# Rotary embedding in a local-attention layer: the two products added by paired transposes into PSUM, and the copy of the last 32 key columns made by ScalarE

## The reference, cut to what matters

```
q, k, v = split(shift(x) @ Wqkv)                  # 16 heads of 64
q = l2norm(q) * q_scale;  k = l2norm(k) * k_scale
q = q * cos * scale + rotate_half(q) * sin * scale
k = k * cos / scale + rotate_half(k) * sin / scale
# windows of 32 tokens; each sees its own keys and those of the window before
sim  = (q @ [k_before, k]^T) * 8, masked;  attn = softmax(sim)
out  = attn @ [v_before, v];  x = out @ Wo + x
```

## Time and profile before

| | |
|---|---|
| median of 3 runs | 5173.48 us (5169.82 to 5185.4) |
| the profiled execution, its own time | 5172.85 us |
| its span, first to last instruction | 5170.8 us |
| PE busy | 3934.8 us (76%) |
| DVE busy | 4374.4 us (85%) |
| ACT busy | 3040.4 us (59%) |
| POOL busy | 2537.9 us (49%) |
| mean granted TensorE clock | 0.913 |

### The profile page before, as it was taken

The page is one execution under the profiler, slowest core; times in us unless marked ns, Lnnn a source line. Parts: engine busy times, 40 slices in busy tenths (PEclk is TensorE's granted clock), DMA queues, the critical chain, the costliest instruction groups (busy, mean ns, idle before and its releaser), DMA issues. The chain is left out here.

```text
span 5170.8 us, 110439 instructions
## 1 busy us (share of the span) xinstructions
PE 3934.8 (76%) x39280; PEld 2903.7 (56%) x39280; DVE 4374.4 (85%) x7725; ACT 3040.4 (59%) x4888; POOL 2537.9 (49%) x1612
## 2 busy tenths in 40 slices
PE   5777777777777777767858678777787787777787
PEld 4655655656656646625535466466465565565565
DVE  8988989979979979954335399799799899898897
ACT  4765756746747747722413477477476476575575
POOL 5645646636636636611010266366366365464562
PEclk8988999989989989986978899899899998899899
DMA  1000000000000000021030000000000000000000
GB/s 47 8 23 11 7 22 12 8 27 6 7 27 7 8 25 8 8 62 26 2 74 1 33 7 7 26 8 21 13 8 20 14 8 19 15 7 22 12 7 12
DMA packets 30608, 88.57 MB, mean 17 GB/s; under 512 B 7505, under 2 KB 13649, under 8 KB 28369
## 3 DMA queue, kind: packets, MB, share of 16 engines
q1 hardware_dynamic: 29104, 80.95, 5.9%
q10 hardware_dynamic: 1152, 3.15, 0.2%
HBM read 38.72 MB, written 1.05 MB: 8 GB/s over the span
## 5 line engine op out<-in xcount | busy, mean ns | idle before, releaser
L771 POOL TENSOR_TENSOR pool<-pool 128x512 f32<-128x512 f32 x768 | 1069.1, 1413 | 968.3 <-DVE pool L869 968.3
L776 POOL TENSOR_TENSOR pool<-pool 128x1024 f32<-128x1024 f32 x384 | 1072.8, 2794 | 168.0 <-DVE pool L880 147.2
L443 PE MATMUL psum<-squares,pool 128*128 128x128 f32 x3072 | 475.4, 304 | 420.8 <-POOL pool L776 259.9
L443 PEld LDWEIGHTS psum<-squares,pool 128*128 128x128 f32 x3072 | 368.9, 153 | 587.2 <-issue 338.1
L880 DVE TENSOR_TENSOR pool<-pool 128x1024 f32<-128x1024 f32 x384 | 678.6, 1806 | 6.8
L483 PE MATMUL psum<-wqkv_hi,xs_lo 128*128 128x512 f32 x1152 | 522.2, 453 | 200.3 <-DVE pool L849 104.6
L646 ACT COPY pool<-psum 64x512 f32<-64x512 f32 x768 | 447.1, 582 | 367.1 <-PE psum L443 361.7
L474 PE MATMUL psum<-pool 128*64 128x128 f32 x6144 | 560.7, 296 | 116.7 <-ACT pool L661 116.5
L420 PE MATMUL psum<-pool 128*128 128x128 f32 x3072 | 455.4, 309 | 130.2 <-ACT pool L646 129.8
L859 DVE TENSOR_REDUCE pool<-pool 128x16 f32<-128x1024 f32 x384 | 449.9, 1210 | 88.1 <-ACT pool L685 88.0
L420 PEld LDWEIGHTS psum<-pool 128*128 128x128 f32 x3072 | 420.4, 219 | 179.4 <-ACT pool L646 167.8
(11 more groups left out here) (165 smaller groups left out, 8247.6 us busy)
## 6 DMA issues: line engine op xcount, KB each, us to landing
pool<-pool SPq DMA_DIRECT2D x192, 128.0 KB, 2.3
pool<-in_wqkv SPq DMA_DIRECT2D x12, 1536.0 KB, 6.0
k_st<-turn_st SPq DMA_DIRECT2D x8, 1536.0 KB, 21.3
pool<-in_wo SPq DMA_DIRECT2D x12, 512.0 KB, 3.6
pool<-in_w SPq DMA_DIRECT2D x12, 341.0 KB, 3.0
pool<-in_w SPq DMA_DIRECT2D x12, 192.0 KB, 2.9
rotary<-in_rotary SPq DMA_DIRECT2D x2, 1024.0 KB, 5.4
pool<-in_scale SPq DMA_DIRECT2D x12, 128.0 KB, 6.2
```

The costliest lines, as they stand in the source:

```text
L443: last = pe.transpose(bank(7 - p % 2)[:, P * j:P * j + P], rot[:, p // 2, 2 * c:2 * c + 2, :], ident)
L771: last = g.tensor_tensor(rot[:, q, :, hd * r:hd * r + hd], qn[:, q, :, hd * (1 - r):hd * (2 - r)], tab, ALU.mult)
L776: g.tensor_tensor(rot[:, q], rot[:, q], by_cos[:, q], ALU.add).then_inc(rot_ready, 1)
```

## The change

The add L776 and the tile `rot` go. GpSimd writes its product to a tile `by_sin`, `by_cos` stays as it was, and TensorE transposes both, the first with `start=True, stop=False` and the second with `start=False, stop=True` on the same 128x128 square of PSUM, so that the square holds the sum. That is 32 transposes in a unit in place of 16. The waits move with it: the transposes wait for `sin_ready` and `cos_ready` in place of `rot_ready`, and VectorE's L880 waits for `t_ready` of the unit before (its transposes of the same half) in place of `rot_ready`. GpSimd's L753 becomes a copy on ScalarE, behind its wait for `t_ready` of `p` = 2 and ahead of the first L646, and GpSimd's `keep` goes, with its wait for `s_ready`.

```diff
                             U = V0 + k
-                            pe.wait_ge(rot_ready, done(U, 2, 0))
+                            pe.wait_ge(sin_ready, done(U, 2, 0))
+                            pe.wait_ge(cos_ready, done(U, 2, 0))
...
-                                    pe.wait_ge(rot_ready, done(U, 2, 1))
+                                    pe.wait_ge(sin_ready, done(U, 2, 1))
+                                    pe.wait_ge(cos_ready, done(U, 2, 1))
...
-                                    last = pe.transpose(bank(7 - p % 2)[:, P * j:P * j + P],
-                                                        rot[:, p // 2, 2 * c:2 * c + 2, :], ident)
+                                    o = bank(7 - p % 2)[:, P * j:P * j + P]
+                                    pe.matmul(o, by_cos[:, p // 2, 2 * c:2 * c + 2, :], ident,
+                                              start=True, stop=False, is_transpose=True)
+                                    last = pe.matmul(o, by_sin[:, p // 2, 2 * c:2 * c + 2, :], ident,
+                                                     start=False, stop=True, is_transpose=True)
...
                                 if p == 2:
+                                    b = kT[k % 2]
+                                    a.copy(b[:, :, :, 0:WIN], b[:, :, :, P:P + WIN]).then_inc(k_kept, 1)
                                     a.wait_ge(k_kept, done(U))
...
-                        def keep(U, k):
-
-                            g.wait_ge(s_ready, done(U - 2))
-                            b = kT[k % 2]
-                            plain(g)
-                            g.tensor_copy(b[:, :, :, 0:WIN], b[:, :, :, P:P + WIN]).then_inc(k_kept, 1)
-
...
-                            if has(1):
-                                keep(U - 1, k - 1)
...
-                                        last = g.tensor_tensor(rot[:, q, :, hd * r:hd * r + hd],
+                                        last = g.tensor_tensor(by_sin[:, q, :, hd * r:hd * r + hd],
                                                                qn[:, q, :, hd * (1 - r):hd * (2 - r)], tab, ALU.mult)
                                     last.then_inc(sin_ready, 1)
-                                    g.wait_ge(sin_ready, done(U, 2, q))
-                                    g.wait_ge(cos_ready, done(U, 2, q))
-                                    g.tensor_tensor(rot[:, q], rot[:, q], by_cos[:, q], ALU.add).then_inc(rot_ready, 1)
...
-                        keep(U0 + UNITS - 1, UNITS - 1)
...
-                                v.wait_ge(rot_ready, done(U - 1, 2, 1))
                                 for q in range(2):
+                                    v.wait_ge(t_ready, done(U - 1, 4, 2 * q + 1))
```

More of the change, by code:

```diff
@@ L61, in macaron_program @@
         sq_ready, qn_ready, cos_ready = sem("sq_ready"), sem("qn_ready"), sem("cos_ready")
-        sin_ready, rot_ready, turn_ready = sem("sin_ready"), sem("rot_ready"), sem("turn_ready")
+        sin_ready, turn_ready = sem("sin_ready"), sem("turn_ready")
         t_ready, t_out, v_out = sem("t_ready"), sem("t_out"), sem("v_out")
@@ L95, in macaron_program @@
                        rb_ready, w1_ready, w2_ready],
-            "scalar": [xs_ready, sq_ready, v_out, t_out, p_ready, pt_ready, o_out, fsq_ready, gel_ready],
+            "scalar": [xs_ready, sq_ready, v_out, t_out, p_ready, pt_ready, o_out, fsq_ready, gel_ready, k_kept],
             "vector": [qn_ready, cos_ready, s_taken, block_ready, y_ready, norm_step, soft_step,
                        xc_ready, diag_ready, xn_ready, hid_ready, x_ready, var_step, aff_step],
-            "gpsimd": [lo_ready, w_hi, w_split, sin_ready, rot_ready, turn_ready, k_kept],
+            "gpsimd": [lo_ready, w_hi, w_split, sin_ready, turn_ready],
         }
@@ L270, in window_half @@
             by_cos = cut(2, HEADS, DH)
-            rot = cut(2, HEADS, DH)
+            by_sin = cut(2, HEADS, DH)
             ss = cut(2 * HEADS)
```

## The result

| | before | after |
|---|---|---|
| median of 4 runs each | 5177.23 us | 4953.28 us (4937.71 to 4975.03) |
| ratio | 1 | 0.957, 95% interval 0.953 to 0.961 |
| span of the profiled execution | 5170.8 us | 4949.2 us |
| DVE, PE, ACT, POOL busy | 4374, 3935, 3040, 2538 us | 4143, 4058, 3174, 1663 us |
| mean granted clock | 0.913 | 0.951 |

Faster by 4.3%, where 2.7% (5033 us) was forecast; the median lies 17 us under the lower end of the range. The lines have other numbers in the kernel after: L869, L880, L771, L846, L849, L859, L896 of before are L863, L874, L769, L840, L843, L853, L890 after; L443 is L446 and L448; L639, L646, L666, L673, L685 are L644, L653, L673, L680, L692; the key copy is L649.

A forecast was written before the change was run, and what follows sets the result against it. VectorE's instruction sequence was taken to bound the kernel. Full steps -8.4, start -5.8 and end +2.5 gave -11.7 us a layer, x12 = -140: 5033 us (-2.7%), range 4970 to 5110.

The forecast's parts named there:

- L145's wait for L776: VectorE's L145, held until GpSimd's sum L776 ends, falls to 0.18 us: -1.6 us a full step.
- the turns: GpSimd's L771 and VectorE's L880 alternate, so L880's pair takes 4.5 us instead of 3.43: +1.1 a full step.
- the start: A layer's first units, without L776's waits: unit 2's L869 comes 5.8 us earlier a layer.
- the slow pace: Transposes at 8 in 1.97 us, as in the layer's second step; unit 0's 32 were priced so.
- A layer's end: GpSimd's weight preparation, which holds VectorE's L896, starts about 2 us later: +2.5 us a layer, bounds 0 and +5.
- it turns out not to be the late one: SyncE's L298 waits on the last unit's `sin_ready`, which was said not to be what delays it.
- the full step: Mid-layer step on VectorE falls from 18.18 to 17.5 us: -0.65 each, -8.4 a layer over 13.
- The spare time of the round: The round through TensorE and ScalarE needs 17.1 us, under VectorE's 17.4 by 0.3 to 0.4.
- The 0.1 us that I added for stretches at the lower clock: Full step: lower-clock stretches can put TensorE back by up to 1.7 us, 0.4 covered; 0.1 added.
- A: Turns fall well: L880's pair stays at 3.43 us, the round bounds at 17.2; 4985 us, chance 0.22.
- B: Slower: transposes at the slow pace make the TensorE and ScalarE round bound at 20.6 us; about 5530 us, chance 0.08.
- C: Nothing moves: L880 takes back L145's gain, its pair at 5.3 us; 5160 to 5180 us, chance 0.08.

The follow-up runs named there:

- the sum alone: The changed kernel with the key copy left on GpSimd, so only the sum in PSUM is new: 4943.05 us, ratio 0.955.
- the late weights: GpSimd's preparation of the next layer's weights made to wait for the first chunk's four diagonals: changed kernel 4940.52 us, kernel before 5137.21 us.
- the two wait experiments: The changed kernel, GpSimd waiting for q's cosine product before k's sine product: 4807.51 us; waiting for both cosine products before its sine products: 4792.83 us.

## Why the prediction was wrong, point by point

**Right: VectorE's sequence bounds, and L145's wait for L776 is what goes.** L145 fell to 0.18 and L152 to its own; the sum alone brings all of it. **Right: the turns.** The pair went from 3.5 to 4.6; taking that back saved 0.86 a step until the next bound. The step was forecast at 17.5 and is 17.52. **Right: the start**, 6.2 us less where 5.8 was forecast. Unit 1 came after 11.2 us for 11.5. One part of its working was wrong without a price: I had the first unit's 32 transposes at the slow pace, and they follow every 0.11 us.

**The step that failed: "A layer's end ... I take +2.5 (bounds 0 and +5)".** Measured -1.8 on ten ends, -8.0 with the global attention, -2.8 in the last: -29 for +30, 59 of the 82 us by which the profiled time fell short. The 8 us at the global attention lie inside the 30 us by which the middle moves anyway; without them it is still the largest part. And GpSimd's block of L304, L309 and L315 stands at ten of the twelve ends alone, not behind the sixth and the last layer, so 5 of the 30 us had nothing to rest on. Three more things in it were wrong.

First, the start of the block. I had the transfer of the weights hang on TensorE's `values` of unit 13 before and after, and so 2 us later. Before, `values` were done 8.2 to 9.8 us after unit 15's L869 and GpSimd's last sine product, which waited behind a sum, only at 11.0: the transfer hung on that one and was issued at 11.3. (The prediction's "it turns out not to be the late one" is wrong for all ten ends.) After, the last sine product is done at 8.6, and now the transfer does hang on `values`: in eight of the ten ends they are done at 9.6 and it is issued at 10.8 (664.20 - 653.45), in the other two they are done at 11.2 and it is issued at 12.4 (1019.50 - 1007.13). So L304, the block's first, begins 18.1 us after L869 in the mean before and 18.3 after, not 2 us later. One of the eight:

```profile
653.45 2.32 DVE L863 TENSOR_TENSOR pool<-psum,pool 128x1024 f32<-128x1024 f32 x2
...
685.55 0.87 DVE L890 TENSOR_SCALAR pool<-squares,pool 128x128 f32<-128x128 f32 x4
```
```profile
664.20 0.34 SPq L298 DMA_DIRECT2D pool<-in_wqkv  x1
```
```profile
671.30 2.74 POOL L304 CAST wqkv_hi<-pool 128x3072 fp32r<-128x3072 f32 x1 [9.29 <-DMA pool<-in_scale]
674.22 5.62 POOL L309 TENSOR_TENSOR wqkv_lo<-pool,wqkv_hi 128x3072 fp32r<-128x3072 f32 x1 [0.18 <-POOL wqkv_hi L304]
679.80 4.50 POOL L315 TENSOR_TENSOR pool<-rotary,pool 128x2048 f32<-128x2048 f32 x1
```

Second, the hold is a race. Here VectorE's L890 came only after all three. In another layer of the same execution, with unit 15's L863 at 1007.13, it began ahead of L304 and was done ahead of L309:

```profile
1007.13 2.32 DVE L863 TENSOR_TENSOR pool<-psum,pool 128x1024 f32<-128x1024 f32 x2
```
```profile
1019.50 0.34 SPq L298 DMA_DIRECT2D pool<-in_wqkv  x1
```
```profile
1026.00 3.38 DVE L890 TENSOR_SCALAR pool<-squares,pool 128x128 f32<-128x128 f32 x4
```

It ended 22 us after L863 and not 33. In three of the ten ends L890's first began before L304 (18.6 to 18.9 us after L863, L304 at 18.7 to 19.4), and all four were done within 28 us; these ends were 93.0 to 96.5 us long, the others 97.7 to 101.6. Before, none of the ten was.

Third, and for the size: I added the block's delay whole. The two kernels with the late weights show that the whole hold of 10 us is worth only 3.1 us before and 2.0 after, so most of it is covered by something behind it, which I did not follow. With the race out of both, the ends are 96.8 and 96.1: the change itself is worth -0.7 there (about what ten ends can tell), not +2.5. The remaining 1.1 is about what the three won races would give: seven holds of ten at 3.1 us are 2.2 in the mean, for the 2.0 measured. That is arithmetic and no test; whether the same ends win in another execution is not shown. For the 6.5 us by which the global attention's untouched code was faster within the middle no cause is shown.

**Mis-sized: the full step**, by 18 us. The later steps are 17.5 as forecast, but the first two of the 13 are 16.4 and 17.3: L880's pair of units 2 and 3 takes 3.66 and 4.33 us in the mean, which is the start's pair and not yet the steady one. That is 1.3 of the 1.5 us a layer. The spare time of the round was 0.85 to 1.1, not 0.3 to 0.4: forecast at 17.1 it is 16.66 where it bounds. A transpose costs 0.11 and not 0.137, and 24 of the 32 stand ahead of the first key copy L653, which came 6.3 us after L843's end and not 6.6. (I had taken 8 transposes' 1.1 us, which holds the last one's own 0.27, as if it were their spacing.) The 0.1 us that I added for stretches at the lower clock had nothing to pay for, since no full step has one.

**The range.** Its lower end allowed the layer's end no gain at all, on the strength of one end of one layer; with -1.8 there it would have reached under 4953.

**Rivals.** A did not come by itself (the pair is 4.65), but its pricing is what the two wait experiments show: VectorE's loss of 1.1 to the turns was real, and without it the round bounds, at 16.66 and not 17.2. B did not come: the clock of the full steps is 1.00. Against the rule of the Trainium skill (TensorE: Matmul & The Clock Gate, Part 4: PE-mode transpose) that transposes do not count as work for the clock gate, the mean clock rose from 0.913 to 0.951 as the transposes doubled, and was 0.945 as they doubled again. The trace cannot say whether they counted or the shorter gaps did; that their pace stayed at 0.11 us decides here. C's condition, a pair of 5.3, was not met (and by the forecast's own terms, starts at -5.8 and ends at +2.5, its time would have been about 5150 and not 5160 to 5180).

## What to carry to other kernels

A tiny VectorE instruction with a long duration was a wait here (0.18 us alone, 1.77 behind L776): look at what GpSimd was doing until its end, and price the removal of the GpSimd instruction by it. When work leaves GpSimd, walk its remaining instructions forward against VectorE's two-input ones: here dropping a wait let them interleave and cost 1.1 us a step, and putting one wait back was worth 146 us. And sum a second resource's round beside the first (here 17.5 against 16.7), since it says both how much of a further gain is real and which edit (here an instruction moved ahead of its neighbour's wait) has to come with it.

## What the runs showed of the hardware

- Accumulating a second fp32 transpose onto the first in PSUM costs what a plain one does: both follow at 0.11 us a 128x128 square (L446 and L448).
- VectorE's and GpSimd's products of two SBUF tiles took turns strictly: L769 of 2.30 us is 1.3 of its own and the rest a wait for L874, and L874 of 2.37 holds such a wait in turn.
- A race between VectorE's short instructions and GpSimd's long ones at a layer's end made ends of the same execution differ by up to 8.6 us (93.0 to 101.6). Whether it is a source of the 37 us between runs of the changed kernel is not shown: with the late weights the runs spread over 12, but those of the sum alone, which has the race too, over 13.
- With 64 transposes in a unit TensorE stood still for over 3 us at each return to the head of its loop in a layer's middle, with no wait in the profile; with 32 it did not.
